# GpSimd's products with C in pairs, and y of both directions summed in the convolution's bank of a selective-scan kernel

## The reference, cut to what matters

```python
def _selective_scan(u, delta, A, Bm, Cm, Dv):
    def step(h, inp):
        u_t, dt_t, B_t, C_t = inp
        dA = jnp.exp(dt_t[:, :, None] * A)
        h = dA * h + (dt_t * u_t)[:, :, None] * B_t[:, None, :]
        y = jnp.einsum('bdn,bn->bd', h, C_t)
        return (h, y)
    ...
    return ys.transpose(1, 0, 2) + u * Dv

xz = (hidden_states @ in_proj_w.T).transpose(0, 2, 1)
x, z = jnp.split(xz, 2, axis=1)
y_fwd = _direction(x, ...)
y_bwd = _direction(x[:, :, ::-1], ...)[:, ::-1, :]
y = (y_fwd + y_bwd) * jax.nn.silu(z.transpose(0, 2, 1))
out = y @ out_proj_w.T
```

## Time and profile before

| | |
|---|---|
| median of 3 runs | 8327.16 us (8322.33 to 8331.08) |
| profiled execution | 8327.64 us, span 8325.9 us |
| PE busy | 7232.1 us (87%) |
| DVE busy | 7202.0 us (87%) |
| POOL busy | 6737.9 us (81%) |
| ACT busy | 5330.5 us (64%) |
| DMA, mean over the span | 101 GB/s |

### The profile page before, as it was taken

One profiled execution on the slowest core, in us unless ns is written; L12 is line 12 of the kernel. 1 busy time (PEld: TensorE's weight loads), 2 busy tenths in 40 slices (PEclk: granted clock), 3 DMA queues, 4 the chain that ended last, 5 costly groups with the idle time before them and its releaser, 6 DMA issues. The chain is left out here.

```text
span 8325.9 us, 116063 instructions
## 1 busy us (share of the span) xinstructions
PE 7232.1 (87%) x32656; PEld 4473.8 (54%) x32656; DVE 7202.0 (87%) x7790; ACT 5330.5 (64%) x12487; POOL 6737.9 (81%) x2833
## 2 busy tenths in 40 slices
PE   7568989998999899977899899899888987779999
PEld 3243555555555555555555555555555555534444
DVE  6921999999999999999999999999999999934444
...
GB/s 86 76 199 135 66 117 69 117 66 117 69 117 66 117 69 117 67 98 43 105 76 127 80 129 75 128 80 127 76 128 81 124 98 82 44 199 139 134 141 75
DMA packets 540822, 843.96 MB, mean 101 GB/s; under 512 B 112576, under 2 KB 260032, under 8 KB 522816
## 3 DMA queue, kind: packets, MB, share of 16 engines
...
HBM read 583.83 MB, written 253.02 MB: 101 GB/s over the span
## 5 line engine op out<-in xcount | busy, mean ns | idle before, releaser
L1179 POOL TENSOR_TENSOR scan_w<-scan_du,scan_bcast_b 128x2048 f32<-128x2048 f32 x1023 | 4633.4, 4541 | 3.6 <-DMA scan_bcast_b<-bc 3.6
L1231 DVE TENSOR_TENSOR_SCAN scan_h<-scan_da,scan_state,scan_w 128x512 f32<-128x512 f32 x2560 | 3178.7, 1280 | 36.6 <-ACT scan_da L1074 21.3
L1074 ACT ACTIVATE scan_da<-scan_delta,scan_prm 128x512 f32<-128x512 f32 x4096 | 2804.3, 685 | 0.0
L962 PE MATMUL scan_yT<-all_ident,scan_hc 128*128 128x128 f32 x10240 | 1514.7, 279 | 768.1 <-DVE scan_hc L1241 767.5
L962 PEld LDWEIGHTS scan_yT<-all_ident,scan_hc 128*128 128x128 f32 x10240 | 1184.8, 142 | 1447.9 <-DVE scan_hc L1241 1068.5
L1231 DVE TENSOR_TENSOR_SCAN scan_hs<-scan_da,scan_state,scan_w 128x512 f32<-128x512 f32 x1536 | 1906.1, 1265 | 59.4 <-PE scan_in_ps L858 41.0
L836 PE MATMUL scan_in_ps<-scan_hn,scan_win 128*128 128x512 f32 x3840 | 1730.8, 593 | 13.5 <-issue 13.5
L1241 DVE TENSOR_TENSOR scan_hc<-scan_h,scan_bcast_c 128x512 f32<-128x512 f32 x2560 | 1652.5, 678 | 38.4 <-ACT scan_state L1054 36.7
L1188 POOL TENSOR_TENSOR scan_hp<-scan_hs,scan_bcast_c 128x512 f32<-128x512 f32 x1024 | 1306.5, 1276 | 60.0 <-issue 54.1
L836 PEld LDWEIGHTS scan_in_ps<-scan_hn,scan_win 128*128 128x128 f32 x3840 | 693.1, 191 | 714.7 <-issue 714.7
L1054 ACT ACTIVATE scan_state<-scan_h 128x1 f32<-128x1 f32 x2560 | 433.4, 169 | 868.6 <-DVE scan_h L1231 861.3
(11 more groups left out here) (128 smaller groups left out, 6761.9 us busy)
## 6 DMA issues: line engine op xcount, KB each, us to landing
...
scan_win<-winx SPq DMA_DIRECT2D x128, 512.0 KB, 3.6
xc<-scan_xc_out SPq DMA_DIRECT2D x256, 256.0 KB, 2.0
scan_xc<-xc SPq DMA_DIRECT2D x256, 256.0 KB, 3.9
...
scan_win<-winz SPq DMA_DIRECT2D x128, 512.0 KB, 4.7
scan_x<-x_pad SPq DMA_DIRECT2D x128, 257.5 KB, 2.6
```

The lines of the kernel that those rows point to most:

```text
L962: last = nc.tensor.matmul(yT[:, tb], hc_slot(b, n)[:, tb * P:(tb + 1) * P], ident[:], is_transpose=True, start=(i == 0 and tb == 0), stop= ...
L1074: nc.scalar.activation(da[:, n % 2], delta[:, s], ACT.Exp, scale=decay(b, n)).then_inc(S["exp_done"], 1)
L1179: nc.gpsimd.tensor_tensor(w[:, g], du[:, s].unsqueeze(1).to_broadcast([P, G, T]), bcast_b[:, g * G:(g + 1) * G], ALU.mult).then_inc(S["w_d ...
L1231: nc.vector.tensor_tensor_scan(flip(b, h_slot(b, n)), flip(b, da[:, n % 2]), flip(b, w[:, n // G, n % G]), state_of(b, n), ALU.mult, ALU.a ...
```

## The change

1. POOL multiplies with C twice a unit in place of four times: states 2 and 5 together, 8 and 11 together, as 128x1024. The pair waits for its second state's scan. POOL's list changes with it.
2. PE takes in both halves of a pair together: at n = 8 and n = 14, where it had them at 5, 8, 11 and 14 (`POOL_AT`). Delta's matmul moves from n = 13 to 14, behind the second pair.
3. `hs` has a slot for each of its six states in place of a ring of four, in the order of `PN + TN`, so that a pair is contiguous. `z_out`, `u` and `du` have one buffer in place of two; `u * D` moves on ACT from n = 10 to n = 5.
4. Backward units store y as before. In each forward unit SP loads the backward y of the same block (`load_y_back`). One unit later PE transposes both into `dt_ps` at n = 11 (`sum_y`, 8 transposes), ACT copies the sum out at n = 13 (`y_copy`), and SP stores it by channels.
5. `stage_out` loads one y and z. POOL's additions and PE's transposes are gone there; DVE reads y from SBUF.

The diff, cut to its core:

```diff
-NHS = 4
+HS = {n: i for i, n in enumerate(PN + TN)}
...
         def h_slot(b, n):
             if n in SN:
-                return hs[:, (b * NSN + SN.index(n)) % NHS]
+                return hs[:, HS[n]]
...
-        POOL_AT = [5, 8, 11, 14]
+        POOL_AT = [8, 8, 14, 14]
...
-        SKIP, DT_AT = 11, 13
+        SKIP, DT_AT, SUM, SUM_COPY = 11, 14, 11, 13
...
+            def load_y_back(b):
+                i = (2 * NCH - 1 - b // DB) * DB + b % DB
+                sp.dma_start(y_back[:], yT_d[i + 1]).then_inc(S["y_loaded"], LOAD)
+
+            def store_y(b):
+                hold(sp, S["y_copied"], b - HALF + 1, S["passed"])
+                sp.dma_start(y_d[ds(b % DB * P, P), ds(t0(b // DB), T)], y_sum[:]).then_inc(S["stored"], LOAD)
...
+            def sum_y(b):
+                pe.wait_ge(S["yT_copied"], b + 2)
+                pe.wait_ge(S["xc_copied"], NU + 2 if b + 1 == NU else min(b + DB + 3, NU) + 2)
+                pe.wait_ge(S["dt_read"], min(b + 3, NU))
+                if b > HALF:
+                    pe.wait_ge(S["y_copied"], b - HALF)
+                for tb in range(TB):
+                    nc.tensor.matmul(dt_ps[:, tb * P:(tb + 1) * P], y_out[:, b % 2, tb], ident[:],
+                                     is_transpose=True, start=(tb == 0), stop=False)
+                pe.wait_ge(S["y_loaded"], (b - HALF + 1) * LOAD)
+                for tb in range(TB):
+                    last = nc.tensor.matmul(dt_ps[:, tb * P:(tb + 1) * P], y_back[:, tb], ident[:],
+                                            is_transpose=True, start=False, stop=(tb == TB - 1))
+                last.then_inc(S["y_mm"], 1)
...
+            def y_copy(b):
+                act.wait_ge(S["y_mm"], b - HALF + 1)
+                if b > HALF:
+                    act.wait_ge(S["stored"], stored_to(b))
+                nc.scalar.activation(y_sum[:], dt_ps[:], ACT.Copy).then_inc(S["y_copied"], 1)
...
             def weigh_c(b, i):
+                first, second = PN[i], PN[i + 1]
...
+                pool.wait_ge(S["scan_done"], b * NS + (second + 1 + SCR))
+                pool.wait_ge(S["hp_used"], b * NP + i + 2)
+                nc.gpsimd.tensor_tensor(hp[:, i:i + 2], hs[:, HS[first]:HS[first] + 2],
+                                        bcast_c[:, first:second + 1:second - first], ALU.mult
+                                        ).then_inc(S["hp_done"], 2)
...
             def unit(b):
                 nxt = b + 1 < NU
                 weigh_b(b, 2)
                 weigh_c(b, 0)
                 weigh_b(b, 3)
-                weigh_c(b, 1)
-                if nxt:
-                    scan_input(b + 1)
-                weigh_c(b, 2)
                 if b % DB == 0:
                     for k in range(NTN):
                         make_diagonal(b, k)
                 if nxt:
+                    scan_input(b + 1)
                     weigh_b(b + 1, 0)
-                weigh_c(b, 3)
+                weigh_c(b, 2)
                 if nxt:
                     weigh_b(b + 1, 1)
...
-                    g = b * NSN + SN.index(n) - NHS
-                    if g >= 0 and SN[g % NSN] in PN:
-                        dve.wait_ge(S["hp_done"], g // NSN * NP + PN.index(SN[g % NSN]) + 1 + NP)
-                    elif g >= 0:
-                        dve.wait_ge(S["h_turn_mm"], g // NSN * NTN + TN.index(SN[g % NSN]) + 1)
+                if n in PN:
+                    dve.wait_ge(S["hp_done"], b * NP + PN.index(n) + 1)
+                elif n in TN and b:
+                    dve.wait_ge(S["h_turn_mm"], (b - 1) * NTN + TN.index(n) + 1)
...
-                    sp.dma_start(yf[:, i], yf_d[ds(c * DB + db + 1, 1)].rearrange("o p t d -> (o p) (t d)")
-                                 ).then_inc(y_loaded[i], LOAD)
-                    sp.dma_start(yb[:, i], yb_d[ds((NCH - 1) * DB + db + 1 - c * DB, 1)]
-                                 .rearrange("o p t d -> (o p) (t d)")).then_inc(y_loaded[i], LOAD)
+                    sp.dma_start(y[:, i], y_d[db * P:(db + 1) * P, ds(c * T, T)]).then_inc(y_loaded[i], LOAD)
                     sp.dma_start(z[:, i], z_d[db * P:(db + 1) * P, ds(c * T, T)]).then_inc(y_loaded[i], LOAD)
...
-            chunks(pe, prepare, project)
+            chunks(pe, lambda c, g, q: None, project)
...
-                    nc.vector.tensor_tensor(yg[:, g, u], yt_ps[:, s], sz[:, slot(q, s)], ALU.mult).then_inc(gated, 1)
+                    nc.vector.tensor_tensor(yg[:, g, u], y[:, slot(q, s)], sz[:, slot(q, s)], ALU.mult).then_inc(gated, 1)
```

105 lines of the change are left out of this document (51 added, 54 removed).

## The result

| | before | changed |
|---|---|---|
| median of 4 runs (lowest to highest) | 8325.5 us (8322.3 to 8331.1) | 8743.6 us (8740.4 to 8746.1) |
| ratio, 95% interval | | 1.0501 (1.0483 to 1.0519) |
| profiled span, mean granted clock | 8325.9 us, 0.948 | 8739.5 us, 0.931 |

The change makes the kernel 5.0% slower. The forecast was 8370 us, at most 8450: the sign is right, the size wrong, and the range too low.

A forecast was written before the change was run, and what follows sets the result against it. DVE's floor, 24.78 us a unit, bounds the kernel; the change closes a ring of 25.5 us a unit. Scan +160 and output stage -117 give +43 on 8327.64: 8370 us, forecast range 8330 to 8410, wider range 8275 to 8450.

The forecast's parts named there:

- a granted clock under 0.95 in the scan: One of three signs named in advance that would show the forecast wrong: TensorE's granted clock in the scan falling below 0.95.
- POOL and the second pair: On POOL: pairs save 0.34 us a unit, worth nothing by itself; the second pair ends 24.3 us into the unit.
- The chain of names: Expected waits: POOL for DVE's scan, TensorE before L953 for POOL, DVE before scans 2, 3, 8 and, forward, 14 for ScalarE's decays.
- Output stage: After the scan: transposes, waits for POOL's sums and a late start go; -117 us, between -73 and -122.
- Units 112 to 127: Backward units without input projection: the wait for a free slot goes, nothing else is late; left at 27.2 us, 0 change.
- the clock as a rival of 0.18 and 8440 us: TensorE's clock falls behind a second wait, up to 1.7 us each time; 8440 us, range 8410 to 8500, chance 0.18.
- the ring's length: Scan 5 through POOL, TensorE and ScalarE to scan 8, by DVE back to scan 5: 51.1 us over two units, 25.5 each.
- delta's path: Late matmuls feeding delta's first step and the copy of `yT` hold scans 2 and 3 about as much; counted in the 25.5.
- the sum of y: Forward units: transposes fit TensorE's spare time; ScalarE's copy delays scan 14 by 0.4 us once in two units, 0.2 a unit.
- the chunk's start: Chunk boundaries: two diagonals of 1.27 us now stand inside the ring, between w and u; 2.5 us a chunk, 0.16 a unit.
- The rule of transposes: TensorE's clock: by the skill transposes don't count as busy like matmuls, so the second wait costs in forward units too; 8440 us.
- HAM oscillation section: Skill section cited for the clock rival: a kernel whose TensorE waits regularly pays for the clock's return at each wait.

The follow-up runs named there:

- singles: Changed kernel with POOL's products with C one by one in their old places: 8448.8 us; with TensorE's sum of y also moved to n = 9: 8176.8 us.
- The run with 5 products of zero: Changed kernel with matmuls adding zero to yT's bank in TensorE's waits, 8 at n = 9 and, at n = 14, 5 backward or 4 forward: 8509.8 us.
- the pairs at n = 15: Changed kernel with TensorE's additions of the second pair at n = 15 in place of 14: 8504.0 us.

## Why the prediction was wrong

The forecast was 373 us too low: 190 in the backward units, 155 in the forward ones, 19 in the last 16, and 9 at the start, in the output stage and between the profiled execution and the median. The forecast's own sign of being wrong, a granted clock under 0.95 in the scan, came (0.94).

**Right.** *POOL and the second pair.* The pair takes 2.36 us and the second ends 24.5 us into a unit that nothing has delayed (forecast 24.3; the step from DVE's scan to GpSimd takes 0.26 us and not 0.1); the pairs' gain on GpSimd is worth nothing. *The chain of names:* GpSimd waits for DVE's scan, TensorE for L953, DVE for ScalarE's decay ahead of scans 2 and 8. The other two places that the forecast named, scans 3 and 14, were not among them: DVE waited ahead of its products of states 1 and 12, for the saves of these states. *Output stage:* from the last scan to the end 112 us less (forecast 117): the projects begin 8.0 us after the weights are asked for in place of 31.3, the weights are asked for 7 us earlier after the last scan (forecast 10), and from the first project to the end it is 82 us less (forecast 83).

**Right by luck.** *Units 112 to 127:* 27.3 us for a forecast of 27.2. I wrote that the wait for a slot goes and that nothing else is late. The wait went, and the second pair, with the fall of the clock behind it, took its place in every second unit; with singles these units take 26.2 us.

**Slips that changed little.** The parts of the output stage add up to 119 us and not 117, and the earlier trace rows has DVE busy 92% in units 112 to 127, not 98 to 99%.

**Wrong, first: the clock as a rival of 0.18 and 8440 us.** I let it fall once in three units at half its cost. It fell in every second backward unit. The price was mis-sized, too: I had "up to 1.7 us each time"; a long and a short unit together take 54.6 us, two units at full clock 52.0, so 2.6, because the slow stretch hits delta's matmul, the turned product, the copy of `yT` and the input projection one behind the other, and three places of DVE each wait for one of them. The run with 5 products of zero puts the clock's share at 27.5 - 26.3 = 1.2 us a unit, 134 us over 112 units, and in the forward half at 27.4 - 26.6 = 0.8 us a unit, some 84 us.

**Second: the ring's length.** I took 51.1 us over two units, 25.5 each, through the input projection and scan 8, and wrote that delta's path holds scans 2 and 3 "about as much". It holds them more: 25.98 us in a single unit. GpSimd's part, from the first pair's start to the second's end, was forecast well (15.85 us, measured 15.90); I closed the ring only over the path that was tight before. Worth 0.5 us a unit, 55 us.

**Third: the sum of y.** The step "scan 14 begins at 21.6 in place of 21.23", halved, 0.2 us a unit. The copy does stand at 20.3 at full clock, as forecast. But I asked which decay stands behind it on ScalarE and not which save: state 12's save at n = 14 holds DVE's product of state 12, which was due 20.2 us into the unit. That is 0.9 us in place of 0.4, and 2.5 when the clock falls behind the wait for state 9, and it is lost in nearly every unit, not once in two. With singles the sum alone makes 2.2 us a unit (27.3 for 25.1) where the forecast gave 0.2. That the sum's place behind TensorE's longest wait is the cause is shown by moving the sum alone: 8449 to 8177 us. The move does two things: the copy no longer waits, and the transposes fill part of the wait behind which the clock fell. With singles, units with the clock up took 26.36 for 24.84, so lateness alone is 1.5 us; the falls made the rest. With the pairs, and the clock held up, a forward unit takes 26.6 us on average for a forecast of 26.0: these 71 us of the 155 are the ring and the copy together. The 19 us of the last 16 units were not taken apart.

**Fourth, perhaps: the chunk's start.** Two diagonals inside the ring: I had 2.5 us a chunk. With the pairs at n = 15 the units of a boundary take 27.0 to 28.6 and 28.3 to 29.7 for 25.1, some 6.5 us a chunk in the backward half, where the kernel before lost about 1. In the changed kernel, whose other units are long too, a boundary costs about the forecast's 2.5. This was not taken apart.

*The rule of transposes.* The prediction cited Part 4 of TensorE: Matmul & The Clock Gate in the Trainium skill, by which transposes don't count as busy in the same way. Here eight transposes in each wait (four in the second one of a forward unit) kept the clock at 0.99, as matmuls did (8504 and 8536 us), so the measurement decides against it for this kernel. Its HAM oscillation section, that a regular wait pays for the clock's return each time, held in part: the kernel paid again and again, but in about every second backward unit and not in each.
